# An attention and feed-forward kernel takes x turned by the host in three of four batches

## The chip, the cores and the metric

The kernel runs on one core of one Trainium2 chip. The metric is the device time of one execution in microseconds. Before the change the median of 3 runs is 2160.63 us (2160.58 to 2162.61). The engines are TensorE (PE; PEld is its weight load), VectorE (DVE), ScalarE (ACT), GpSimd (POOL) and SyncE (SP, which here only issues DMAs).

## The reference

x is 4 batches of 512 rows of 1024. Each batch attends to itself and to 64 rows of context, and a feed-forward block with a router follows. Cut to what matters here:

```python
m = jnp.mean(x, axis=-1, keepdims=True)            # _layernorm, per row of x
v = jnp.var(x, axis=-1, keepdims=True)
z = (x - m) / jnp.sqrt(v + 1e-5)
q = z @ Wq.T                                       # 16 heads of 96
hidden = jnp.concatenate([context, z], axis=1)
k, v = hidden @ Wk.T, hidden @ Wv.T                # 4 key and value heads of 96
x = x + softmax(q k^T / sqrt(96)) v @ Wo.T
x = x + ffn(layernorm(x))                          # up, relu^2, down; a routed low-rank path
```

Mean and root belong to a row of x, that is to a token.

## The kernel before

TensorE contracts over partitions, so z must stand with features on partitions and tokens along the free dimension. Every product is made of three fp32r matmuls (`parts3`, lines 116 to 118) of operands split in a high and a low part; for z these are `zhi` and `zlo`, 8 chunks (k) of 128 features by 512 tokens.

The program runs in stages: p0 (weights are split, the context is projected, batch 0 is normalized), a (projections of each batch), b (attention), c, d and e. The change is in stage a. There, for each batch, PE makes 19 output chunks (A_EV): 3 of k and 12 of q, each 128x512, in five groups of three (k index outside, chunk inside), and then 4 value tiles t of 128x384. A group uses three PSUM banks, and two sets of banks alternate. Each chunk n is evicted by ACT (`a_hi_out`, line 527) and DVE (`a_lo_out`, line 532) into one of two staging slots and stored by SP (`a_store`, line 547). ACT waits until the slot's last stores have landed.

z of batch b + 1 is made inside batch b. SP loads x (2 MB, line 153) early in batch b, with tokens on partitions. Ahead of chunk 9's eviction DVE takes statistics, the root (with ACT's square root) and scales x in place to z (lines 177 to 198). PE turns z in 8 blocks of four 128x128 transposes (`pe_t`, line 210): two blocks ahead of value tile 2 and the other six behind the k steps 2 to 7 of value tile 3. ACT copies each turned bank to zhi (line 219), once the last reader of that part of zhi has passed (semaphore `a_zfree`), and DVE makes zlo (line 223). ACT and DVE do k = 0 to 6 ahead of the last chunk's (18) eviction and k = 7 behind it. PE's next batch waits for zlo of each k, and its second chunk waits until chunk 18 is evicted, whose bank it takes. Each engine's order is written out by hand, and semaphores alone tie the engines together.

In the names of the tiles, "operands" holds weights, zhi, zlo and one staging slot, "staging" holds x, raw weights and the other slot, "small" holds statistics.

## Time and profile before

| what | us |
|---|---|
| median of 3 runs | 2160.63 |
| profiled execution, its own time | 2160.62 |
| its span | 2158.8 |
| PE busy | 2129.8 (99%) |
| DVE busy | 804.3 (37%) |
| ACT busy | 692.2 (32%) |
| POOL busy | 698.7 (32%) |

The span runs from the first to the last instruction of the profiled execution. Matmuls are pipelined: the start of one to the start of the next is its cost, and the duration shown is longer. In stage a, POOL has no instruction from 100 to 350 us.

### The profile page before, as it was taken

The page shows a single profiled execution, that of the slowest core. Times are in us where ns is not written, and L with a number is a line of the kernel's source. Part 1 is how long each engine was busy: PE and PEld are TensorE (multiplying, and loading weights), DVE is VectorE, ACT ScalarE, POOL GpSimd, SP SyncE. Part 2 cuts the span into 40 slices and gives each one's busy share as a digit, 9 for nine tenths or more (in the row PEclk, how much of TensorE's full clock was granted, in tenths as well). Part 3 has the DMA queues.
Part 4 walks back from the last instruction along what each step waited for, and adds up shares of the span by engine and source line. Part 5 has one row for each costly group of instructions (what it writes and reads, how often), then busy time and mean ns, then how long its engine had stood idle before and what let it go on. Part 6 is the DMA issues. An engine that isn't in the chain of part 4 may idle for free.

```text
span 2158.8 us, 30561 instructions
## 1 busy us (share of the span) xinstructions
PE 2129.8 (99%) x9820; PEld 1752.6 (81%) x9820; DVE 804.3 (37%) x1407; ACT 692.2 (32%) x1201; POOL 698.7 (32%) x572
## 2 busy tenths in 40 slices
PE   7999999999999999999999999999999999999998
PEld 6888888887777777878888878788888888888886
DVE  4223222167777778850100313232221132222222
ACT  4111111047777777761111223211123311111111
POOL 3500000126777767672222434010004422222221
PEclk9999999999999999999999999999999999999999
DMA  4732322525556556534333535322114532222222
GB/s 165 233 127 107 126 97 88 164 85 140 141 144 162 136 134 156 131 96 149 134 119 119 187 103 173 110 78 97 63 66 138 188 109 81 86 84 88 84 87 72
DMA packets 230940, 261.62 MB, mean 121 GB/s; under 512 B 76496, under 2 KB 144336, under 8 KB 230736
## 3 DMA queue, kind: packets, MB, share of 16 engines
q1 hardware_dynamic: 186016, 188.70, 28.6%
q10 hardware_dynamic: 44848, 71.97, 10.9%
q8 instruction: 40, 0.66, 0.1%
q14 instruction: 36, 0.29, 0.1%
HBM read 168.07 MB, written 92.27 MB: 121 GB/s over the span
## 4 chain that ended last, share of the span: by engine, by line
PE 97%; DVE 1%; DMA 1%; issue 1%; ACT 0%; POOL 0%; SPq 0%; DVEq 0%; ACTq 0%; POOLq 0%
PE psum L116 30%; PE psum L117 29%; PE psum L118 29%; PE psum L865 3%; PE psum L210 1%; PE psum L916 1%; PE psum L917 1%; PE psum L900 1%; PE psum L899 1%; DMA staging<-in_wqkv 1%; PE psum L1530 0%; PE psum L1529 0%; PE psum L872 0%; DVE staging L198 0%; DMA staging<-in_ctx 0%
## 5 line engine op out<-in xcount | busy, mean ns | idle before, releaser
L116 PE MATMUL psum<-operands 128*128 128x512 f32 (+3 forms) x2888 | 1125.0, 390 | 12.2 <-DVE operands L325 9.1
L117 PE MATMUL psum<-operands 128*128 128x512 f32 (+3 forms) x2888 | 1111.1, 385 | 0.0
L118 PE MATMUL psum<-operands 128*128 128x512 f32 (+3 forms) x2888 | 1109.7, 384 | 0.0
L116 PEld LDWEIGHTS psum<-operands 128*128 128x128 f32 (+1 forms) x2888 | 543.9, 188 | 119.4 <-DVE operands L325 10.2
L118 PEld LDWEIGHTS psum<-operands 128*128 128x128 f32 (+1 forms) x2888 | 544.3, 188 | 106.7
L117 PEld LDWEIGHTS psum<-operands 128*128 128x128 f32 (+1 forms) x2888 | 545.2, 189 | 92.9
L1158 POOL TENSOR_TENSOR operands<-staging,operands 128x512 fp32r<-128x512 f32 x92 | 118.3, 1296 | 367.7 <-ACT operands L1153 367.4
L1044 DVE TENSOR_REDUCE small<-psum 128x1 f32<-128x576 f32 x256 | 192.1, 750 | 99.7 <-PE psum L865 99.7
L1757 POOL TENSOR_TENSOR operands<-operands 128x640 fp32r<-128x640 f32 x64 | 100.6, 1578 | 318.8 <-ACT operands L1752 318.7
L786 POOL TENSOR_TENSOR operands<-staging,operands 128x512 fp32r<-128x512 f32 x128 | 164.0, 1289 | 36.1 <-ACT operands L966 27.3
L1609 DVE TENSOR_TENSOR staging<-staging 128x512 f32<-128x512 f32 x64 | 46.0, 738 | 304.3 <-ACT staging L1575 303.5
L1752 ACT ACTIVATE operands<-operands 128x640 fp32r<-128x640 f32 x64 | 47.3, 740 | 282.4 <-DMA operands<-h_scratch 282.4
L1344 POOL TENSOR_TENSOR operands<-operands 128x384 fp32r<-128x384 f32 x64 | 66.0, 1037 | 183.1 <-ACT operands L1339 182.5
L779 POOL MEMSET operands<- 64x32 f32 (+7 forms) x22 | 8.6, 389 | 350.4 <-PE psum L118 349.3
L959 ACT ACTIVATE staging<-psum 128x512 f32<-128x512 f32 (+1 forms) x192 | 109.3, 588 | 39.4 <-DVE psum L1072 33.0
L865 PEld LDWEIGHTS psum<-operands 96*128 96x128 f32 x512 | 91.0, 189 | 33.6 <-DVE small L1044 17.9
L865 PE MATMUL psum<-operands 96*128 96x288 f32 x512 | 116.2, 309 | 0.3 <-DVE small L1044 0.3
L966 ACT ACTIVATE operands<-staging 128x512 fp32r<-128x512 f32 (+1 forms) x192 | 112.9, 620 | 0.0
L788 POOL TENSOR_TENSOR operands<-staging,operands 64x512 fp32r<-64x512 f32 x64 | 82.5, 1288 | 74.0 <-ACT operands L966 70.4
L1153 ACT ACTIVATE operands<-staging 128x512 fp32r<-128x512 f32 x92 | 56.3, 629 | 140.0 <-DMA staging<-in_up_w 57.7
L1575 ACT ACTIVATE staging<-psum 128x512 f32<-128x512 f32 x80 | 46.5, 597 | 165.2 <-PE psum L118 159.7
L532 DVE SCALAR_TENSOR_TENSOR staging<-psum,staging 128x512 fp32r<-128x512 f32 (+1 forms) x40 | 26.5, 664 | 192.5 <-ACT staging L527 192.5
(102 smaller groups left out, 1363.6 us busy)
## 6 DMA issues: line engine op xcount, KB each, us to landing
h_scratch<-staging ACTq DMA_DIRECT2D x80, 256.0 KB, 2.1
operands<-h_scratch SPq DMA_DIRECT2D x64, 320.0 KB, 3.1
operands<-recip_scratch SPq DMA_DIRECT2D x64, 192.0 KB, 4.1
o_scratch<-staging SPq DMA_DIRECT2D x64, 192.0 KB, 4.8
operands<-o_scratch SPq DMA_DIRECT2D x64, 192.0 KB, 2.7
operands<-q_hi_scratch ACTq DMA_DIRECT2D x14, 768.0 KB, 5.9
operands<-q_lo_scratch ACTq DMA_DIRECT2D x14, 768.0 KB, 5.8
staging<-in_x SPq DMA_DIRECT2D x20, 512.0 KB, 3.9
```

Of the source, the lines that this page charges most:

```text
L116: e.matmul(o, lh, rh, start=first, stop=False)
L117: e.matmul(o, lh, rl, start=False, stop=False)
L118: return e.matmul(o, ll, rh, start=False, stop=last)
L786: e.tensor_tensor(pt[j][1], pst[j // 2], raw(pt[j][0]), ALU.subtract).then_inc(b_lop, 1)
L788: e.tensor_tensor(pt[j][0][C:P], pst[j // 2][0:C], raw(pt[j][0][0:C]), ALU.subtract).then_inc(b_lop, 1)
L865: m = e.matmul(bank[:, h * TH:(h + 1) * TH], qp[p][0][0:HD, a * S + u * P:a * S + (u + 1) * P], kp[p][0][0:HD, h * TH:(h + 1) * TH], start ...
L959: e.activation(pst[j // 2][0:n], bank[0:n], ACT.Exp).then_inc(b_ex, 1)
L966: e.activation(pt[j][0][0:n], pst[j // 2][0:n], ACT.Copy).then_inc(b_hia, 1)
L1044: e.tensor_reduce(nm[o % 2][:, u:u + 1], bank[:, 0:T], AX.X, ALU.max, negate=True).then_inc(b_mx, 1)
L1158: e.tensor_tensor(job_part(j, h, slot_lo), halves[h], raw(job_part(j, h, slot_hi)), ALU.subtract).then_inc(j_lo, 1)
L1344: e.tensor_tensor(cu[u][1], raw(cu[u][1]), raw(cu[u][0]), ALU.subtract).then_inc(cc_lo, 1)
L1757: e.tensor_tensor(eu[u][1], raw(eu[u][1]), raw(eu[u][0]), ALU.subtract).then_inc(e_lo, 1)
```

## The change

The host hands over a second copy of x, `xt`, with features on partitions (128 partitions, 8 chunks k, 512 tokens). Batch 0 is made as before. For batches 1 to 3:

- x is still loaded with tokens on partitions, four neighbouring tokens to each partition, and DVE takes mean and root from it. It no longer scales x, but copies the mean to its own place (line 199 of the changed kernel).
- SP, behind chunk 9's stores, loads the batch's part of `xt` (2 MB) over x and stores the mean and the root (2 KB each) to DRAM. Behind chunk 10's stores it waits for these to land and loads them back spread over all partitions (MR, 128x1024).
- GpSimd subtracts the mean and multiplies by the root in place, 16 operations of 128x512.
- ACT makes zhi (line 499) and DVE makes zlo (line 503) from there; PE does no turning.

```diff
@@ -148,15 +149,15 @@
             def load(e, src, b):
-                e.wait_ge(*past(zt, b * DK))
+                e.wait_ge(*past(zl if tiles else zt, b * DK))
                 e.sem_inc(idle, 1)
-                e.dma_start(xn, src[bass.ds(b * S, S), :].rearrange("(t p) d -> p t d", p=P)).then_inc(ld, 16)
+                e.dma_start(xn, src[bass.ds(b * S, S), :].rearrange("(p t) d -> p t d" if tiles else "(t p) d -> p t d", p=P)).then_inc(ld, 16)
             def load_tile(e, src, t):
                 e.dma_start(xn[:, t, :], src[t * P:(t + 1) * P, :]).then_inc(ld_t[t], 16)
-            def dve_norm(e, b, by_tile=None):
+            def dve_norm(e, b, by_tile=None, z=True):
                 n = [0]
                 def link(ins, last=True):
@@ -194,9 +195,12 @@
                 link(e.tensor_scalar(n1, n1, -0.5, 1.5, ALU.mult, ALU.add))
                 link(e.tensor_tensor(rstd, n1, rt, ALU.mult))
                 assert n[0] == LN_CHAIN
+                if not z:
+                    e.tensor_copy(mean, mv[:, :, 0]).then_inc(cp, 1)
+                    return
                 for t in range(ST):
-                    z = e.tensor_scalar(xn[:, t, :], xn[:, t, :], mv[:, t, 0:1], rstd[:, t:t + 1], ALU.subtract, ALU.mult)
-                z.then_inc(zn, 1)
+                    m = e.tensor_scalar(xn[:, t, :], xn[:, t, :], mv[:, t, 0:1], rstd[:, t:t + 1], ALU.subtract, ALU.mult)
+                m.then_inc(zn, 1)
             def act_sqrt(e, b, to=rt):
                 e.wait_ge(*past(ch, b * LN_CHAIN + 14))
@@ -269,6 +273,11 @@
         c_stage = [tuple(mmf(10 * SLOT + (2 * c + i) * BC, BC) for i in range(2)) for c in range(KC)]
         c_stage += [tuple(mmf(11 * SLOT + (2 * t + i) * KVE, KVE) for i in range(2)) for t in range(2)]
         stage = [tuple(SF[:, STG + i * NB:STG + (i + 1) * NB].bitcast(f32r) for i in range(2)), (mmf(GWO, NB), mmf(GWO + NB, NB))]
+        XT = SF[:, 0:DK * S].rearrange("p (k s) -> p k s", k=DK)
+        mean = sm[:, 320:320 + ST]
+        MR = SF[:, STG + 2 * NB:STG + 4 * NB]
+        a_ms, a_mr, a_xt = sem("a_moments_stored", 32), sem("a_moments_spread"), sem("a_x_turned")
+        a_sub, a_mul = sem("a_mean_off"), sem("a_normalized", DK)
         c_mm, c_sh, c_ev, c_st = (sem(f"ctx_{n}") for n in ("product", "staged_hi", "staged", "stored"))
         v_w = [MM[:, 15 * SLOT:18 * SLOT].rearrange("p (c h k e) -> p h k c e", c=KC, h=2, k=DK)[:, i] for i in range(2)]
         v_rows = [t.rearrange("(q s) d -> q s d", s=T) for t in v_d]
@@ -440,8 +449,58 @@
         A_GROUPS = [[QC, QC + 1, QC + 2]] + [[3 * g, 3 * g + 1, 3 * g + 2] for g in range(QC // 3)]
         NQK = QC + KC
         A_EV = NQK + ST
-        a_load, a_load_tile, a_norm, a_sqrt, a_pet, a_hi, a_lo, a_zl, a_fr, a_zt = norm_z(
+        a_load, a_load_tile, a_norm, a_sqrt, a_pet, a_hi, a_lo, a_zl, a_fr, a_zt, a_zh, a_ch, a_cp = norm_z(
             "a", XN, lambda e, b: e.wait_ge(*past(a_acc, b * A_EV)), (5, 6, 7), True)
+
+        A_CP = 1
+
+        def a_moments_out(e, b):
+
+            e.wait_ge(*past(a_ch, b * LN_CHAIN + 2 * ST))
+            e.sem_inc(idle, 1)
+            e.dma_start(XT, xt.rearrange("b p k s -> (b p) k s")[bass.ds(b * P, P)]).then_inc(a_xt, 16)
+            e.wait_ge(*past(a_ch, b * LN_CHAIN + LN_CHAIN))
+            e.sem_inc(idle, 1)
+            e.wait_ge(*past(a_cp, b + A_CP))
+            e.sem_inc(idle, 1)
+            for q, src in enumerate((mean, rstd)):
+                e.dma_start(m_d[q * S:(q + 1) * S].rearrange("(p t) -> p t", t=ST), src).then_inc(a_ms, 16)
+
+        def a_moments_in(e, b):
+
+            if isinstance(b, int):
+                e.wait_ge(*past(w_lop, len(BY_POOL) + 2 * QC))
+            e.wait_ge(*past(a_mul, b * DK - DK))
+            e.sem_inc(idle, 1)
+            e.wait_ge(*past(a_ms, b * 32))
+            e.sem_inc(idle, 1)
+            e.dma_start(MR, m_d.partition_broadcast(P)).then_inc(a_mr, 16)
+
+        def a_pool(e):
+            def take_mean(k):
+                e.tensor_tensor(XT[:, k, :], XT[:, k, :], MR[:, 0:S], ALU.subtract).then_inc(a_sub, 1)
+
+            with e.Fori(1, B) as b:
+                e.wait_ge(*past(a_xt, b * 16))
+                e.wait_ge(*past(a_mr, b * 16))
+                take_mean(0)
+                for k in range(DK):
+                    if k + 1 < DK:
+                        take_mean(k + 1)
+                    e.wait_ge(*past(a_sub, b * DK + (k + 1 - DK)))
+                    e.tensor_tensor(XT[:, k, :], XT[:, k, :], MR[:, S:2 * S], ALU.mult).then_inc(a_mul, 1)
+
+        def a_hi_next(e, b, k):
+            e.wait_ge(*past(a_mul, b * DK + (k + 1 - DK)))
+            if k < DK - 1:
+                e.wait_ge(*past(a_fr, (b - 1) * (DK - 1) + k + 1))
+            else:
+                e.wait_ge(*past(a_acc, b * A_EV))
+            e.activation(zhi[:, k, :], XT[:, k, :], ACT.Copy).then_inc(a_zh, 1)
+
+        def a_lo_next(e, b, k):
+            e.wait_ge(*past(a_zh, b * DK + k + 1))
+            e.tensor_tensor(zlo[:, k, :], XT[:, k, :], raw(zhi[:, k, :]), ALU.subtract).then_inc(a_zl, 1)
         def a_sp(e):
             more = [[13], [14, 15, 16], [17, 18], [19, 20], [21, 22], [23]]
@@ -449,6 +508,10 @@
                 a_store(e, 0, n)
                 if n == 3:
                     a_load(e, x_r, 1)
+                if n == 9:
+                    a_moments_out(e, 1)
+                if n == 10:
+                    a_moments_in(e, 1)
                 for k in [NF + q for q in (more[n] if n < len(more) else [])]:
                     c, h = LATER[k - NF]
                     if (c, h) == (8, 0):
@@ -482,9 +549,6 @@
                     g, c = t // 2, t % 2
                     if c == 0:
                         e.wait_ge(*past(a_ev, b * A_EV + 3 * (len(A_GROUPS) - 1 + g)))
-                    if t == ST - 2 and not last:
-                        a_pet(e, b + 1, 0)
-                        a_pet(e, b + 1, 1)
                     for k in range(DK):
                         zt_ = [z[:, k, t * P:(t + 1) * P] for z in (zhi, zlo)]
                         m = parts3(e, PS[:, 3 * ((g + 1) % 2) + c, 0:KVE], zt_[0], zt_[1],
@@ -495,8 +559,6 @@
                             m.then_inc(a_acc, 1)
                         elif t == ST - 1:
                             m.then_inc(a_fr, 1)
-                        if t == ST - 1 and k >= 2 and not last:
-                            a_pet(e, b + 1, k)
             e.wait_ge(*past(c_ev, KC))
             with e.Fori(0, B - 1) as b:
@@ -553,13 +615,13 @@
                         a_sqrt(e, b + 1)
                     if n == A_EV - 1 and not last:
                         for k in range(DK - 1):
-                            a_hi(e, b + 1, k)
+                            a_hi_next(e, b + 1, k)
                     a_hi_out(e, b, n)
                     if n == A_EV - 3 and last:
                         e.wait_ge(*past(ph_start, 2))
                         e.activation(sm[:, 336:337], ident[:, 0:1], ACT.Exp)
                 if not last:
-                    a_hi(e, b + 1, DK - 1)
+                    a_hi_next(e, b + 1, DK - 1)
             with e.Fori(0, B - 1) as b:
                 body(b, False)
@@ -569,15 +631,16 @@
             def body(b, last):
                 for n in range(A_EV):
                     if n == 9 and not last:
-                        a_norm(e, b + 1)
+                        e.wait_ge(*past(a_ms, b * 32))
+                        a_norm(e, b + 1, z=False)
                     if n == A_EV - 1 and not last:
                         for k in range(DK - 1):
-                            a_lo(e, b + 1, k)
+                            a_lo_next(e, b + 1, k)
                     a_lo_out(e, b, n)
                     if last and NQK <= n < A_EV - 1:
                         b_dve_first(e, n - NQK + 1)
                 if not last:
-                    a_lo(e, b + 1, DK - 1)
+                    a_lo_next(e, b + 1, DK - 1)
             with e.Fori(0, B - 1) as b:
                 body(b, False)
@@ -2003,6 +2067,7 @@
     arrays = {
         "x": inputs["x"],
+        "xt": np.asarray(inputs["x"]).reshape(-1, 512, 8, 128).transpose(0, 3, 2, 1),
         "ctx": in_rows(np.asarray(inputs["ctx_4096"]).reshape(-1, inputs["ctx_4096"].shape[-1]).T, 1).reshape(128, 8, -1),
         "wqkv": in_chunks(np.concatenate([np.asarray(inputs[_P + w]) for w in ("Wq", "Wk", "Wv")], axis=0).T),
         "wo": np.asarray(inputs[_P + "Wo"]).T,
```

On PE, at the end of a batch's loop body, before. Tile 3's k steps end in blocks of turns of the z in "staging", each waiting for the PSUM bank (`a_zlo`); L502 is the loop's branch:

```order
L116 MATMUL psum<-operands 128x384
L117 MATMUL psum<-operands 128x384
L118 MATMUL psum<-operands 128x384
L208 REGISTER_ALU
L210 MATMUL psum<-ident,staging 128x128 [waits a_zlo]
L210 MATMUL psum<-ident,staging 128x128 x3
L502 REGISTER_ALU
L502 COMPARE_AND_BRANCH
```

And in the changed kernel, where the products that follow are the next group's first chunks (512 wide); the second chunk's first product waits for the evictions alone (`a_staged`):

```order
L117 MATMUL psum<-operands 128x384
L118 MATMUL psum<-operands 128x384
L119 MATMUL psum<-operands 128x384
L564 REGISTER_ALU
L564 COMPARE_AND_BRANCH
L117 MATMUL psum<-operands 128x512 [waits a_staged,a_zlo]
L118 MATMUL psum<-operands 128x512
L119 MATMUL psum<-operands 128x512
L117 MATMUL psum<-operands 128x512 [waits a_staged]
```

Eight blocks of turns per body are gone, two of them ahead of tile 2, and nothing stands in their place.

On DVE, at the same place, before: chunk 17's eviction and the first zlo, seven of which stand there ahead of chunk 18's eviction:

```order
L532 SCALAR_TENSOR_TENSOR operands<-psum,operands 128x384 [waits a_staged_hi]
L222 ISA
L223 TENSOR_TENSOR operands<-psum,operands 128x512 [waits a_zhi]
L222 REGISTER_ALU
L223 TENSOR_TENSOR operands<-psum,operands 128x512 [waits a_zhi]
```

And in the changed kernel:

```order
L594 SCALAR_TENSOR_TENSOR operands<-psum,operands 128x384 [waits a_staged_hi]
L502 ISA
L503 TENSOR_TENSOR operands<-staging,operands 128x512 [waits a_zhi]
L502 REGISTER_ALU
L503 TENSOR_TENSOR operands<-staging,operands 128x512 [waits a_zhi]
```

The order is the same; the subtraction reads x from "staging" where it read a PSUM bank.

On GpSimd, between the weight split and stage b, a loop body over batches 1 to 3 is new. Its start (L481 takes the mean off, L491 multiplies by the root):

```order
L481 TENSOR_TENSOR staging<-staging 128x512 [waits a_moments_spread,a_x_turned]
L481 TENSOR_TENSOR staging<-staging 128x512
L490 ISA
L491 TENSOR_TENSOR staging<-staging 128x512 [waits a_mean_off]
L481 TENSOR_TENSOR staging<-staging 128x512
L490 REGISTER_ALU
L491 TENSOR_TENSOR staging<-staging 128x512 [waits a_mean_off]
```

It begins with both loads' landing; the multiplication for k stands one subtraction behind its own. ACT's zhi for k waits for it (`a_normalized`).

## Rows read from the trace of the kernel before

**Rows 1.** The page, part 4: the chain that ended last, by engine.
```profile
PE 97%; DVE 1%; DMA 1%; issue 1%; ACT 0%; POOL 0%; SPq 0%; DVEq 0%; ACTq 0%; POOLq 0%
```

**Rows 2.** PE in order of time: start, duration, engine, line, count [idle before].
```profile
235.07 1.03 PE L210 MATMUL psum<-ident,staging 128*128 128x128 f32 x8
235.86 0.42 PE L116 MATMUL psum<-operands 128*128 128x384 f32 x1
...
240.11 0.33 PE L116 MATMUL psum<-operands 128*128 128x384 f32 x1
...
240.63 0.33 PE L116 MATMUL psum<-operands 128*128 128x384 f32 x1
...
247.52 0.61 PE L210 MATMUL psum<-ident,staging 128*128 128x128 f32 x4
248.06 0.49 PE L116 MATMUL psum<-operands 128*128 128x512 f32 x1
...
249.12 0.50 PE L116 MATMUL psum<-operands 128*128 128x512 f32 x1
```

**Rows 3.** DVE in order of time, statistics and turnover of the same batch.
```profile
206.22 2.98 DVE L198 TENSOR_SCALAR staging<-staging,small 128x1024 f32<-128x1024 f32 x4 [0.15 <-DVE small L195]
...
240.91 0.56 DVE L532 SCALAR_TENSOR_TENSOR operands<-psum,operands 128x384 fp32r<-128x384 f32 x1 [4.48 <-ACT operands L527]
241.46 1.29 DVE L223 TENSOR_TENSOR operands<-psum,operands 128x512 fp32r<-128x512 f32 x2
```

**Rows 4.** SP in order of time: stores of chunks 9 and 11.
```profile
211.25 0.38 SPq L547 DMA_DIRECT2D q_lo_scratch<-operands  x1
...
215.08 0.33 SPq L547 DMA_DIRECT2D q_hi_scratch<-operands  x1
```

**Rows 5.** DMA issues of the whole span: count, KB each, median us to landing.
```profile
staging<-in_x SPq DMA_DIRECT2D x3, 2048.0 KB, 7.9
q_hi_scratch<-staging SPq DMA_DIRECT2D x24, 256.0 KB, 2.1
...
staging<-in_gamma SPq DMA_DIRECT2D x1, 512.0 KB, 4.7
staging<-in_beta SPq DMA_DIRECT2D x1, 512.0 KB, 4.2
```

**Rows 6.** DMA issues between 74 and 90 us.
```profile
staging<-in_x SPq DMA_DIRECT2D x1, 2048.0 KB, 11.0
...
q_hi_scratch<-staging SPq DMA_DIRECT2D x1, 256.0 KB, 9.3
```

**Rows 7.** POOL in order of time, two operations with DVE quiet.
```profile
1603.56 2.55 POOL L1158 TENSOR_TENSOR operands<-staging,operands 128x512 fp32r<-128x512 f32 x2 [28.34 <-ACT operands L1153]
```

**Rows 8.** POOL and DVE in order of time, in stage p0.
```profile
19.20 8.38 POOL L325 TENSOR_TENSOR operands<-staging,operands 128x512 fp32r<-128x512 f32 x6 [14.10 <-ACT operands L320]
...
23.64 5.21 DVE L198 TENSOR_SCALAR staging<-staging,small 128x1024 f32<-128x1024 f32 x4
```

**Rows 9.** Line 1704 (ns min/median/max), and POOL and DVE beside it.
```profile
L1704 DVE TENSOR_TENSOR operands<-staging,operands x12: 677/692/2070, 1720.8 to 1735.5; 128x512 fp32r<-128x512 f32 x12
...
1719.34 3.57 POOL L1757 TENSOR_TENSOR operands<-operands 128x640 fp32r<-128x640 f32 x2 [4.64 <-ACT operands L1752]
...
1720.78 8.15 DVE L1704 TENSOR_TENSOR operands<-staging,operands 128x512 fp32r<-128x512 f32 x8 [4.93 <-ACT operands L1698]
```

**Rows 10.** Line 1067, subtractions from PSUM in stage b (ns min/median/max).
```profile
L1067 DVE TENSOR_TENSOR operands<-psum,operands x128: 691/692/692, 459.0 to 959.1; 128x512 fp32r<-128x512 f32 x128
```

**Rows 11.** PE after idles; then slices: us, PE, PEld, DVE, ACT, POOL busy, PEclk, DMA, GB/s.
```profile
23.13 0.41 PE L116 MATMUL psum<-operands 128*128 128x384 f32 x1 [2.00 <-POOL operands L325]
...
28.91 2.82 PE L210 MATMUL psum<-ident,staging 128*128 128x128 f32 x12 [3.46 <-DVE staging L198]
...
28.00:30.00 2.00, 1.09 (x5) 1.09 (x6) 0.85 (x2) 0.00 (x0) 0.00 (x0) 0.53 0.08 25
...
34.00:36.00 2.00, 2.00 (x14) 1.87 (x12) 0.88 (x3) 0.78 (x2) 0.00 (x0) 0.76 0.00 0
```

More of the change, by code:

```diff
@@ L3, with xattn_ffn_kernel @@
 from contextlib import ExitStack
-def xattn_ffn_kernel(nc, x, ctx, wqkv, wo, gate_w, up_w, down_w, fc1_w, fc2_w, expert_w, gamma, beta, out):
+def xattn_ffn_kernel(nc, x, xt, ctx, wqkv, wo, gate_w, up_w, down_w, fc1_w, fc2_w, expert_w, gamma, beta, out):
     f32 = mybir.dt.float32
@@ L53, in xattn_ffn_kernel @@
     w_d = dram("fold_scratch", (L, D))
+    m_d = nc.dram_tensor("moments_scratch", (2 * S,), f32, kind="Internal").ap()
     x_r = x.rearrange("b s d -> (b s) d")
@@ L223, in dve_lo @@
                 e.tensor_tensor(zlo[:, k, :], z_bank(b, k), raw(zhi[:, k, :]), ALU.subtract).then_inc(zl, 1)
-            return load, load_tile, dve_norm, act_sqrt, pe_t, act_hi, dve_lo, zl, fr, zt
+            return load, load_tile, dve_norm, act_sqrt, pe_t, act_hi, dve_lo, zl, fr, zt, zh, ch, cp
         def mm_groups(e, b, groups, lo_sem, wait_bank, slot_of, done, slot_ready=None, after_group=None, free=None, pe_t=None):
@@ L463, in a_sp @@
                     a_store(e, b, n)
+                    if n == 9:
+                        a_moments_out(e, b + 1)
+                    if n == 10:
+                        a_moments_in(e, b + 1)
         def a_pe(e):
@@ L1207, in xattn_ffn_kernel @@
         d_acc = sem("d_product", 20)
-        d_load, _, d_norm, d_sqrt, d_pet0, d_hi, d_lo, d_zl, d_fr, d_zt = norm_z(
+        d_load, _, d_norm, d_sqrt, d_pet0, d_hi, d_lo, d_zl, d_fr, d_zt, _, _, _ = norm_z(
             "d", XN2, lambda e, b: e.wait_ge(*past(d_acc, b * ND)))
@@ L1930, in _ @@
             a_sp(e)
-            e.wait_ge(*past(a_zt, B * DK))
+            e.wait_ge(*past(a_zl, B * DK))
             e.sem_inc(idle, 1)
@@ L1948, in _ @@
             p0_pool(e)
+            a_pool(e)
             b_pool(e)
```

## The prediction, on record before the changed kernel ran

> **What bounds the kernel now.** I read the chain of waits first: PE is 97% of what ended last [rows 1]. So a change pays only where it takes matmuls away or ends a PE wait, and costs where it makes one. Next I read PE's order of time at a turnover from one batch to the next, the second of the three (loop index 1 to 2, near 240 us) [rows 2], then DVE's at the same place [rows 3]. In them the reader is to see a tight hand-over. PE turns z between its last value products (line 210); ACT copies the turned bank to zhi and DVE subtracts it to zlo; then chunk 18, the batch's last value product, is evicted by ACT and DVE, and the next batch's second chunk may overwrite its bank. That chunk's first product stands at 249.12 us. All times below are of this turnover unless said; the other two repeat it. The profiled execution took 2160.62 us around a span of 2158.8, and the median of the runs is 2160.63, so the sum is made on 2160.6.
>
> **What goes.** PE loses 8 blocks of 4 turns per turnover, 96 turns over three. The first two blocks stand at 235.07 and the products resume at 235.86: 0.79 us, and 0.88 with the slower first product behind them. The value products step 0.52 us per k (240.11, 240.63) [rows 2]. Without turns the last tile (t = 3) starts at 240.11 - 0.88 = 239.2, ends 8 x 0.52 later at 243.4, and the first chunk of the next batch takes its three products with the loop's branch in about 0.9 us (now under 1.25: the last block of turns starts at 247.52, takes 0.36, and 249.12 is the second chunk) [rows 2]. PE therefore reaches the second chunk at 244.3 instead of 249.12. That is the whole possible gain: 4.8 us, 14.5 for three. DVE also loses four 128x1024 scalings, 2.98 us [rows 3], but those lie under products of group 3, where DVE idles; I cost that at nothing.
>
> **What comes.** GpSimd takes 16 operations of 128x512 per batch (8 subtractions of the mean, 8 multiplications by the root); ACT's and DVE's split now reads x from SBUF, not PSUM. When can GpSimd start? DVE has the moments at about 206.4, when now its scaling begins at 206.22 [rows 3], before chunk 9 is evicted. SP issues chunk 9's second store at 211.25 (0.38 us) [rows 4], then the turned x at 212.0. A load of 2 MB lands 7.9 us after its issue [rows 5]: 219.9. The two stores of the moments stand right behind it on the same queue. Behind such a load a store of 256 KB took 9.3 us [rows 6], where that kind's median is 2.1 [rows 5]; so I let the small ones land just after the load, 220.3. SP issues the spread at 220.6. It moves 512 KB, as gamma's (4.7 us) and beta's (4.2) [rows 5]; the middle gives 225.05, so GpSimd starts at 225.1. Two of its operations back to back took 2.55 us, 1.25 for the pace after the first [rows 7]: operation n ends at 225.15 + 1.25n. The multiplication for k is operation 2k + 3, and k = 7's is the 16th, at 245.15.
>
> **Where it meets DVE.** Chunk 17's eviction on DVE stands at 240.91 now [rows 3]; 0.88 earlier, 0.55 us long, it lets DVE ask for its first zlo at 240.6. GpSimd then is in operation 13 of 16. Now DVE reads PSUM and zhi, one SBUF operand, and 128 such subtractions beside a busy GpSimd never took over 692 ns [rows 10]. The new one reads x and zhi, both SBUF. The kernel before has this very form in its last stage: twelve of them took 692 ns in the median and 2070 at most, and beside GpSimd operations eight took 8.15 us and two GpSimd ones 3.57 instead of 3.1 [rows 9]. At the start four DVE scalings took 5.21 us beside GpSimd [rows 8] against 2.98 alone [rows 3], while six GpSimd operations took 8.38, not 7.6. So the two engines take turns there: DVE waits out a GpSimd operation, GpSimd then about 0.5 us of DVE. Worked through:
> - DVE 0 waits to 241.4 and is done at 241.9; GpSimd 14 to 243.15; DVE 1 to 243.65; GpSimd 15 to 244.9; DVE 2 to 245.4; GpSimd 16 to 246.65; DVE 3 to 247.15.
> - GpSimd is out. DVE 4 to 6 go at the pace of the pair in [rows 3], 1.29 less 0.69: 0.60 each, 248.95. Chunk 18's eviction adds 0.55: 249.5.
> ACT is not late: k = 6 is multiplied at 244.9. PE's second chunk starts at 249.5 instead of 249.12: all 4.8 us are gone and 0.4 more. Bounds from the same rows: no blocking gives -3.4 us (below), and rows spread 2.5 us later give +2.7.
>
> The Trainium skill (SBUF — State Buffer, Who interferes with whom) says that a VectorE instruction with two SBUF inputs contends with a GpSimd instruction that reads SBUF, and that whoever issues first has the shared ports for the whole instruction. The trace agrees on the contention [rows 9]. Taken alone the rule would also allow a steady GpSimd to keep DVE out until its 16th operation: then DVE starts at 245.15 and PE at 249.85, 0.7 us late instead of 0.4. The 8.38 us of [rows 8] speak for taking turns, so the sum uses that.
>
> **The new idle time and PE's clock.** Now [rows 2] show no idle of note here. After, PE stands from 244.3 to 249.5, 5.2 us at one stretch. Near 21 us an idle of 2.00 left the next products at full pace; one of 3.46, ending at 28.91, came with a granted clock of 0.53 in the slice 28 to 30 and 0.76 in 34 to 36 [rows 11], so the half level (1.2 GHz of 2.4) held from 28.1 to about 35.0. PE worked 6.1 us at it and lost half: 3.0 us. A stall of 5.2 us is longer than the one that did this, so I take 3.0 us per turnover; bounds 0 (clock stays) and 3.0.
>
> **Waits added elsewhere.** SP waits for the moments' stores after chunk 10. Behind it stand chunk 11's stores, at 215.08 now [rows 4] and at about 221 then. Who waits for those is ACT's eviction of chunk 13, a whole group of 72 products later; nothing is lost unless the load takes over 6 us more. ACT waits for each multiplication with chunk 18's eviction queued behind; that is in the sum. GpSimd's loop lies between its weight split and stage b's fills; DVE's wait for the old stores of moments was met a batch ago. Turned x overwrites x only once the statistics are read. These I cost at nothing; what the added 6 MB of loads cost is in the landing times.
>
> **Sum.** Three turnovers at 0.4 + 3.0 = 3.4 us: +10.2. 2160.6 + 10.2 = 2170.8, so 2171.
>
> **Rivals.**
> 1. The spread rows come later (the small stores or the spread take 2.5 us more behind chunk 10's stores). GpSimd starts at 227.6 and is in operation 11 when DVE asks; five turns instead of three, PE at 251.85: +2.7, and the clock's 3.0. Three times 5.7: 2177.7. For it: the one queue carries all this.
> 2. As forecast, but the clock holds. 3 x 0.4: 2161.8. For it: only one long idle in the middle of work is there to read. Against: it was the shorter one.
> 3. The other side, faster: DVE is not kept out, since its subtraction proceeds beside GpSimd's. Then ACT's k = 6 waits for operation 15 (243.9), is done at 244.5, DVE at 245.1, chunk 18 at 245.7; PE is 3.4 us early and idles 1.5, too short for the clock. 3 x -3.4: 2150.5. Against it [rows 9].
> 4. Also faster: the small stores overtake the 2 MB. The Trainium skill's page DMA: Bandwidth & Descriptors (Queues, rings and completion order) says that completion is not in order per issuing engine; it also says that each DMA engine takes descriptors in ring order, and the 9.3 us of [rows 6] agree with that part. As a mechanism here: the moments land within some 2 us of their issue, the spread shares the load's time and lands near 221.5; GpSimd's 16th operation ends at 241.55, DVE runs free from there (0.5 + 6 x 0.6 + 0.55), PE resumes at 246.25, 2.9 us early with 2 us of idle. 3 x -2.9: 2152. The sign flips where the rows are spread before about 223: each microsecond there is nearly one at PE, and the clock comes or stays with it.
>
> **Chances.** Forecast 0.60, rival 1 0.17, rival 2 0.10, rival 3 0.07, rival 4 0.06. This kernel's measurement tells about 0.2%, 4.3 us. Faster is rivals 3 and 4: 0.13. Within 0.2% is rival 2: 0.10. Slower is the rest: 0.77. The range runs from rival 2's place less its error, 2160, to rival 1's with some more, 2180; outside lie rivals 3 and 4 and some 0.04 beyond rival 1.
>
> **What would show it.** In the profile after: no turns on PE between 40 and 360 us (line 214 there); DVE's line 503 with seven per turnover, the first three or four 1.2 to 1.8 us each while GpSimd's lines 481 and 491 stretch from 1.29 to about 1.75; GpSimd starting some 13 us after the load's issue; one PE idle of 4.5 to 6 us per turnover ended by DVE's eviction (line 594); a granted clock of 0.5 for some microseconds after it, three times. Wrong would be: line 503 flat at 0.69, GpSimd done before 240.6 on this scale, PE idle under 2.5 us, or a clock that stays at 1.00.

## The result, and the profile after

The changed kernel takes 2173.06 us (median of 5 runs, 2170.58 to 2177.88), against 2160.58 us for the kernel before on the same chip (5 runs, 2157.89 to 2162.61): ratio 1.0064, 95% interval 1.0053 to 1.0075. The change makes the kernel 0.6% slower. Its profiled execution took 2175.06 us around a span of 2173.2.

The chain of waits of the changed kernel, against [rows 1]:

```profile
PE 94%; DVE 2%; DMA 1%; issue 1%; ACT 1%; POOL 0%; DVEq 0%; SPq 0%; ACTq 0%; POOLq 0%
```

PE gave up three points of the chain. The waits of PE (line waited for: us in total, times, longest) name whom it waits for:

```profile
PE psum L117 <- DVE staging L594: 12.9, 3, 7.6
PE psum L117 <- DVE operands L334: 9.0, 6, 6.2
PE psum L117 <- DVE operands L503: 6.7, 2, 3.7
```

Line 334 is line 325 of the kernel before, which had 9.1 us there. The other two, five waits and 19.6 us, all stand at the turnovers: 594 is DVE's eviction, here of chunk 18, and 503 the new subtraction. PE in order of time at the first turnover (columns as in [rows 2]):

```profile
140.09 0.39 PE L117 MATMUL psum<-operands 128*128 128x512 f32 x1
...
140.56 0.40 PE L119 MATMUL psum<-operands 128*128 128x512 f32 x1
148.57 0.80 PE L117 MATMUL psum<-operands 128*128 128x512 f32 x1 [7.62 <-DVE staging L594]
149.16 0.63 PE L118 MATMUL psum<-operands 128*128 128x512 f32 x1
```

and at the second, the one of [rows 2]:

```profile
252.96 0.49 PE L117 MATMUL psum<-operands 128*128 128x512 f32 x1 [3.69 <-DVE operands L503]
...
253.53 0.55 PE L119 MATMUL psum<-operands 128*128 128x512 f32 x1
256.96 0.80 PE L117 MATMUL psum<-operands 128*128 128x512 f32 x1 [2.88 <-DVE staging L594]
```

The reader is to see two things. The transposes are gone, and in their place PE stands idle: at the first turnover once, 7.62 us before the second chunk; at the second twice, 3.69 us before the first chunk, whose first zlo is late, and 2.88 before the second chunk (at the third 3.04 and 2.43). And the products behind the idle last longer: 0.63 us where 0.40 stood. Two windows of equal length, one right after the other (busy time and count of each engine, then granted clock, DMA share, GB/s), show what that costs:

```profile
148.60:154.60 6.00, 6.00 (x14) 4.80 (x15) 0.51 (x1) 0.00 (x0) 0.00 (x0) 0.50 0.85 273
154.70:160.70 6.00, 6.00 (x28) 4.96 (x27) 0.00 (x0) 0.00 (x0) 0.00 (x0) 1.00 0.30 128
```

PE is busy in both, at 1.2 GHz with 14 products, at 2.4 GHz with 28.

DVE at the first turnover, against [rows 3]:

```profile
136.73 0.56 DVE L594 SCALAR_TENSOR_TENSOR operands<-psum,operands 128x384 fp32r<-128x384 f32 x1 [3.60 <-ACT operands L589]
137.31 10.73 DVE L503 TENSOR_TENSOR operands<-staging,operands 128x512 fp32r<-128x512 f32 x7
147.97 0.54 DVE L594 SCALAR_TENSOR_TENSOR staging<-psum,staging 128x384 fp32r<-128x384 f32 x1
```

Seven subtractions take 10.73 us. Six of them took 1.75 to 1.77 each, the seventh, with GpSimd done, 0.68. GpSimd beside them:

```profile
137.22 1.30 POOL L491 TENSOR_TENSOR staging<-staging 128x512 f32<-128x512 f32 x1
138.47 1.74 POOL L481 TENSOR_TENSOR staging<-staging 128x512 f32<-128x512 f32 x1
140.17 1.71 POOL L491 TENSOR_TENSOR staging<-staging 128x512 f32<-128x512 f32 x1
```

The two engines take turns here. SP and its landings set when GpSimd starts (SP in order of time at the second turnover, against [rows 4]):

```profile
217.70 0.36 SPq L461 DMA_DIRECT2D staging<-in_xt  x1
218.38 0.81 SPq L467 DMA_DIRECT2D moments_scratch<-small  x2
...
227.74 0.33 SPq L477 DMA_DIRECT2D staging<-moments_scratch  x1
```

To measure a turnover I use two marks: the start of a batch's first value product (128x384), and the first product of the second chunk of the next batch. Before, the value products start at 123.25, 226.73, 330.17 and 433.62, and the second chunk 22.4 us behind each. After, they start at 123.43, 232.45, 339.63 and 447.49, so the turnovers cost 5.54, 3.74 and 4.41 us, 13.7 in all. The second chunk (148.57, 256.96, 363.59) is late against the 22.4 by 2.7, 2.1 and 1.6 us; the remaining 2.8, 1.6 and 2.9 come behind it, while the clock is halved. The profiled execution lies 2.0 us above the median of its runs, so the marks give 13.7 us where the medians give 12.5.

### The profile page after: what moved, and what is told of

It is laid out like the page before. It is cut to its first block, busy times and chain, and to the rows that moved or that the text cites. A ratio compares the mean times of both kernels' runs of the same rounds, so it can differ in the third digit from the quotient of the medians.

```text
span 2173.2 us, 30459 instructions
## 1 busy us (share of the span) xinstructions
PE 2126.0 (98%) x9724; PEld 1748.6 (80%) x9724; DVE 811.1 (37%) x1398; ACT 692.0 (32%) x1201; POOL 760.4 (35%) x620
## 4 chain that ended last, share of the span: by engine, by line
PE 94%; DVE 2%; DMA 1%; issue 1%; ACT 1%; POOL 0%; DVEq 0%; SPq 0%; ACTq 0%; POOLq 0%
PE psum L117 29%; PE psum L118 29%; PE psum L119 28%; PE psum L928 3%; PE psum L214 1%; DMA q_lo_scratch<-operands 1%; PE psum L979 1%; PE psum L980 1%; PE psum L963 1%; PE psum L962 1%; DVE operands L503 1%; DMA staging<-in_wqkv 0%; PE psum L1593 0%; PE psum L1592 0%; PE psum L935 0%
## 5 line engine op out<-in xcount | busy, mean ns | idle before, releaser
L481 POOL TENSOR_TENSOR staging<-staging 128x512 f32<-128x512 f32 x24 | 32.1, 1343 | 197.7 <-DMA staging<-moments_scratch 197.7
```

## The experiments

The times of the kernel before beside the first four are 2159.76 (2158.15 to 2161.15), beside the next four 2160.01 (2158.23 to 2161.02). "Idle" is PE's longest at a turnover by the waits.

**Without GpSimd.** Nothing normalizes x; ACT and DVE wait for the load alone. Its lines 501 and 592 are 503 and 594 of the changed kernel.

```diff
-            e.wait_ge(*past(a_mul, b * DK + (k + 1 - DK)))
+            e.wait_ge(*past(a_xt, b * 16))
...
-            a_pool(e)
```

> The changed kernel with GpSimd's loop left out: ACT and DVE split x as it was loaded, so z is not normalized in batches 1 to 3 (this leaves work out). All loads, stores and the statistics stay. Theory: GpSimd is the whole loss, through its late results and through keeping DVE off; then DVE's seven splits run free, PE reaches the second chunk 3 to 3.5 us earlier than before the change, idles about 1.5 us and keeps its clock: about 2150.5 us. Rival: the loss is in reading x from SBUF or in the added loads and SP's waits: 2160 or more.

2148.3 us (2147.72 to 2150.47), ratio 0.9948 [0.9934, 0.9961]: 2 us under what I had expected. DVE in order of time:

```profile
234.25 4.30 DVE L501 TENSOR_TENSOR operands<-staging,operands 128x512 fp32r<-128x512 f32 x7
```

and PE:

```profile
237.03 0.39 PE L117 MATMUL psum<-operands 128*128 128x512 f32 x1
...
239.07 0.50 PE L117 MATMUL psum<-operands 128*128 128x512 f32 x1 [1.18 <-DVE staging L592]
```

Seven subtractions take 4.30 instead of 10.73 us, the idle is 1.2, the clock stays at 1.00 from 110 to 380 us, and a batch takes 99.75 us where before took 103.45. All of the loss hangs on GpSimd, and so do the 3.7 us per turnover that the missing transposes can give. This run alone can't say whether GpSimd's lateness or its use of SBUF does it.

**Data apart.** ACT and DVE split rows of the weights in place of x; GpSimd's work goes on beside them, and neither waits for it (only SP does, before it loads the next batch's x).

```diff
-            e.wait_ge(*past(a_mul, b * DK + (k + 1 - DK)))
...
-            e.tensor_tensor(zlo[:, k, :], XT[:, k, :], raw(zhi[:, k, :]), ALU.subtract).then_inc(a_zl, 1)
+            e.tensor_tensor(zlo[:, k, :], raw(slot_hi(k)[:, 0:NB]), raw(zhi[:, k, :]), ALU.subtract).then_inc(a_zl, 1)
```

> The changed kernel, where GpSimd does its 16 operations at the same times on the turned x, but nobody waits for them: ACT and DVE split other data in SBUF (parts of the weights, so the output is not that of the reference). Theory (DVE is kept off while GpSimd reads SBUF): DVE's first splits of a turnover still take several us, PE's idle stays 5 to 8 us and its clock halves, 2169 to 2176 us. Rival (GpSimd's results are late, and ACT waits for them): DVE's splits take 0.68 us and the time falls to about 2150.

2172.11 us (2170.99 to 2177.16), ratio 1.0067 [1.0053, 1.008]. DVE in order of time:

```profile
136.03 9.73 DVE L502 TENSOR_TENSOR operands<-operands 128x512 fp32r<-128x512 f32 x7
```

and GpSimd:

```profile
136.16 1.75 POOL L481 TENSOR_TENSOR staging<-staging 128x512 f32<-128x512 f32 x1
137.87 1.75 POOL L491 TENSOR_TENSOR staging<-staging 128x512 f32<-128x512 f32 x1
```

With no wait between them, four or five subtractions per turnover still take 1.74 to 1.79 us, PE idles 6.9 us at most and the clock halves three times. Contention while both run is enough for the whole loss; that GpSimd's results are late is not needed for it. What late results would cost without the contention is not shown: no run has the one without the other.

**Three chunks earlier.** Statistics, load, stores and spread move from chunks 9 and 10 to 6 and 7, on SP, ACT and DVE.

```diff
-                if n == 9:
+                if n == 6:
-                if n == 10:
+                if n == 7:
```

> The changed kernel with statistics, the turned load and the moments' stores at chunk 6 and the spread at chunk 7, one group (16.3 us) earlier, nothing else. Theory: GpSimd is through about 10 us before tile 3, so neither late results nor shared access remain: each turnover gains 3 to 3.5 us against the kernel before, 2150 to 2152 us, with no slice at half clock there. Rival: loads at that time hold up the stores of chunks 6 to 8 and PE's banks: over 2155.

2148.98 us (2148.43 to 2149.5), ratio 0.9951 [0.9937, 0.9964], 1 us under the range that I gave. The last two GpSimd operations before the second turnover:

```profile
221.50 2.54 POOL L491 TENSOR_TENSOR staging<-staging 128x512 f32<-128x512 f32 x2
```

and DVE:

```profile
234.18 4.30 DVE L503 TENSOR_TENSOR operands<-staging,operands 128x512 fp32r<-128x512 f32 x7
```

GpSimd is done 10 us before DVE asks, and the kernel is as fast as without GpSimd. GpSimd starts 16.3 us ahead of the batch's value products here (204.0 against 220.3), instead of about at them; the same work is free there. At the first turnover it starts 7.6 us ahead, and that was enough too: the batch takes the same 99.76 us.

**Filler.** 20 products into an unused bank behind the value products keep PE busy where it would stand. It tells the clock's share.

```diff
+                if not last:
+                    for i in range(20):
+                        e.matmul(PS[:, 7, :], slot_hi(QC)[:, 0:P], slot_hi(QC + 1)[:, 0:NB], start=True, stop=True)
```

> The changed kernel with 20 single matmuls of 512 columns (4.5 us) into an unused bank behind each of the first three batches' last value product, whose results nobody reads. They fill most of the stall. Theory: the half clock is about 8.5 of the 12.5 us lost (6.05, 3.5 and 7.5 us of PE's work at half level in the profile after). The clock stays full in the two shorter stalls at least, and the time falls to 2163 to 2167. Rival: the clock doesn't matter or falls anyway, and the fillers add where the stall is shorter than they are: 2173 or more.

2168.2 us (2166.32 to 2170.05), ratio 1.0041 [1.0027, 1.0054]: between what I had expected and the rival. PE at the first turnover:

```profile
146.26 0.50 PE L117 MATMUL psum<-operands 128*128 128x512 f32 x1 [2.28 <-DVE staging L597]
...
146.83 0.40 PE L119 MATMUL psum<-operands 128*128 128x512 f32 x1
```

PE in order of time, second turnover:

```profile
243.98 4.74 PE L564 MATMUL psum<-operands 128*128 128x512 f32 x20
...
251.21 0.50 PE L117 MATMUL psum<-operands 128*128 128x512 f32 x1 [1.81 <-DVE staging L597]
...
251.82 0.63 PE L119 MATMUL psum<-operands 128*128 128x512 f32 x1
```

and three windows, one per turnover:

```profile
140.00:160.00 20.00, 17.72 (x79) 14.33 (x78) 6.81 (x7) 1.89 (x4) 4.59 (x3) 1.00 0.36 125
245.00:262.00 17.00, 15.19 (x61) 12.06 (x60) 6.75 (x7) 1.64 (x3) 3.93 (x3) 0.90 0.40 147
350.00:368.00 18.00, 16.57 (x74) 13.42 (x73) 7.89 (x8) 2.28 (x4) 5.07 (x3) 1.00 0.12 25
```

The clock now holds at two turnovers of three, the first and the third, and the turnovers cost 1.9, 3.1 and 1.2 us against before: 6.2 instead of 13.7. That is 7.5 less in the traces, but the medians gained only 4.9. The second chunk is late by 2.0, 1.5 and 1.1 us here, which is 1.8 less in all than in the changed kernel. What comes behind it is 0.0, 1.6 and 0.0 instead of 2.8, 1.6 and 2.9: where the clock holds, this part is gone, 5.7 us. So the halved clock follows what PE does in the gap, not the absence of the transposes. The length of an idle alone does not tell which level comes: 2.28 us at the first turnover and 1.43 at the third left the clock full, 1.81 at the second did not. Why is open.

**Moments first.** The two small stores stand ahead of the load of x.

```diff
-            e.dma_start(XT, xt.rearrange("b p k s -> (b p) k s")[bass.ds(b * P, P)]).then_inc(a_xt, 16)
...
+            e.dma_start(XT, xt.rearrange("b p k s -> (b p) k s")[bass.ds(b * P, P)]).then_inc(a_xt, 16)
```

> The changed kernel with one exchange on SP: the two small stores of mean and root are issued ahead of the 2 MB load of turned x instead of behind it. Theory (the end of GpSimd's work against the turnover decides): the small stores no longer wait out the load (they landed 8.5 us after issue), the spread is issued right behind chunk 10's stores, shares the queue with the load, and lands about 2 us behind it: GpSimd starts about 11 us after the load's issue instead of 14 to 15.6, DVE meets its last two operations at most, PE idles about 3 us: each turnover 1 to 2 us ahead of the kernel before if the clock holds: 2154 to 2158. Rival (order of the small stores doesn't matter, since the queue finishes them with the load anyway): within 2 us of the changed kernel, 2171 to 2175.

2169.95 us (2169.59 to 2171.08), ratio 1.0046 [1.0033, 1.006]: I was wrong by 12 us or more. DMA issues between 105 and 125 us (count, KB each, us to landing), this kernel:

```profile
staging<-in_xt SPq DMA_DIRECT2D x1, 2048.0 KB, 9.2
...
staging<-moments_scratch SPq DMA_DIRECT2D x1, 512.0 KB, 9.2
moments_scratch<-small SPq DMA_DIRECT2D x2, 2.0 KB, 2.4
```

and the changed kernel, same stretch:

```profile
staging<-in_xt SPq DMA_DIRECT2D x1, 2048.0 KB, 10.5
...
staging<-moments_scratch SPq DMA_DIRECT2D x1, 512.0 KB, 4.4
moments_scratch<-small SPq DMA_DIRECT2D x2, 2.0 KB, 8.5
```

The small stores land in 2.4 us instead of 8.5, as I had expected; but now the spread is issued while the load runs and takes 9.2 us instead of 4.4. GpSimd starts 11.9 us after the load's issue in the first turnover instead of 15.6, and 11.5 instead of 14.6 in the second. Part of that is given back, since the load itself is issued later: 13.7 us ahead of the value products instead of 14.75 in the second turnover, behind the small stores. (In the first the load's place varies from trace to trace of the changed kernel, 14.3, 12.1 and 12.5 us ahead; here it is 11.8.) In its batch GpSimd starts 1.3, 2.1 and 1.4 us sooner than in the first trace of the changed kernel. PE still idled 4.5 to 6.5 us, with the clock halved three times.

**A busy GpSimd beside the kernel before.** 20 multiplications of 128x512 per turnover (line 456) run beside DVE's old subtraction.

```diff
+                e.wait_ge(*past(a_acc, b * A_EV + NQK))
+                for j in range(20):
...
+                    e.tensor_tensor(SF[:, to:to + NB], raw(slot_hi(13)[:, 0:NB]), raw(slot_hi(14)[:, 0:NB]), ALU.mult).then_inc(a_busy, 1)
```

> The kernel before the change, with 20 GpSimd multiplications of 128x512 added at each of the three turnovers (from chunk 14's product on), which read weights and write to unused room in SBUF. DVE's splits read PSUM there. Theory (only a DVE operation with two operands in SBUF is kept off): DVE's line 223 stays at 0.69 us and the time is that of before, within 1.5 us: 2158 to 2162. Rival (GpSimd's mere activity in the turnover slows DVE or PE): 2165 or more.

2159.8 us (2159.08 to 2160.84), ratio 1.0000 [0.9991, 1.0009]. Groups of instructions (busy, mean ns, idle before):

```profile
L456 POOL TENSOR_TENSOR staging<-operands 128x512 f32<-128x512 f32 x60 | 74.9, 1294 | 181.0 <-PE psum L118 181.0
L223 DVE TENSOR_TENSOR operands<-psum,operands 128x512 fp32r<-128x512 f32 x64 | 43.4, 689 | 55.6 <-ACT operands L219 55.6
```

and the same two groups of the changed kernel, where DVE reads two operands from SBUF:

```profile
L491 POOL TENSOR_TENSOR staging<-staging 128x512 f32<-128x512 f32 x24 | 32.4, 1360 | 0.0
L503 DVE TENSOR_TENSOR operands<-staging,operands 128x512 fp32r<-128x512 f32 x24 | 32.4, 1407 | 0.1
```

With one operand in PSUM neither engine notices the other (689 and 1294 ns). It is the change of DVE's operand, not GpSimd's work as such, that makes them meet.

**Eviction sooner.** As three chunks earlier, and chunk 18's eviction stands behind four splits instead of seven.

```diff
-                        for k in range(DK - 1):
+                        for k in range(4):
...
-                    a_lo_next(e, b + 1, DK - 1)
+                    for k in range(4, DK):
+                        a_lo_next(e, b + 1, k)
```

> The kernel of e3 (all of the added work one group earlier) with chunk 18's eviction moved on ACT and DVE from behind the split of k = 6 to behind that of k = 3. Theory: the idle of 1.36 us that e3 still has at each turnover is DVE's chain of seven splits ahead of that eviction; with four ahead, the eviction waits for PE's product itself and PE idles about 0.5 us: 0.9 us less each, 2146 to 2147 against e3's 2149. Rival (zlo of k = 4 to 7, now later, holds PE up in turn): no gain or a loss.

2148.03 us (2146.04 to 2150.32), ratio 0.9942 [0.9928, 0.9955], 1 us above the range that I gave. PE:

```profile
240.72 0.51 PE L117 MATMUL psum<-operands 128*128 128x512 f32 x1 [0.55 <-DVE staging L594]
```

The idle falls from 1.19 to 0.55 us, the batch from 99.75 to 99.1.

**Second chunk last.** In addition PE takes the second chunk after the third at the first k of the first group.

```diff
-                    for c, ch in enumerate(chunks):
+                    for c, ch in [list(enumerate(chunks))[q] for q in ((0, 2, 1) if swap and g == 0 and k == 0 else (0, 1, 2)[:len(chunks)])]:
```

> The kernel of e7 where PE, in a batch's first group, takes at k = 0 the third chunk before the second, whose bank is the last to be evicted. Theory: 0.7 us of products cover what idle e7 leaves; the three turnovers have no idle, 1 to 1.5 us less than e7 in all: 2144.5 to 2146.

2147.01 us (2145.7 to 2149.71), ratio 0.9942 [0.9928, 0.9955]: 13 us under the kernel before, and again 1 above the range that I gave. A batch takes 98.45 us, 5.0 less than before. No idle is left at the turnovers. In the medians the last two steps (1 us each) lie within the spread of the runs; only the marks in the traces show them apart.

**The changed kernel twice more.** In its first trace the second turnover read otherwise than the first. DVE and GpSimd, this trace:

```profile
246.34 10.11 DVE L503 TENSOR_TENSOR operands<-staging,operands 128x512 fp32r<-128x512 f32 x7
```

```profile
246.03 1.32 POOL L481 TENSOR_TENSOR staging<-staging 128x512 f32<-128x512 f32 x1
247.28 1.32 POOL L491 TENSOR_TENSOR staging<-staging 128x512 f32<-128x512 f32 x1
248.53 1.31 POOL L481 TENSOR_TENSOR staging<-staging 128x512 f32<-128x512 f32 x1
249.76 2.52 POOL L491 TENSOR_TENSOR staging<-staging 128x512 f32<-128x512 f32 x2
```

GpSimd is hardly slowed; DVE's first subtraction took 6.50 us, its end 0.56 behind that of GpSimd's last operation, and the others 0.68. The third was the same, with 5.93.

> The changed kernel once more, for a second trace. Open is why in its first trace VectorE and GpSimd took turns in the first turnover (six subtractions of 1.75 us) and VectorE was kept out in the other two (first subtraction 6.50 and 5.93 us, then 0.68 each). Theory A, it is the moment at which VectorE asks that decides, which varies by a fraction of a microsecond from execution to execution: then the pattern changes, kept out in another number or other places of the three, and the time lies within 2170 to 2178 us. Theory B, it is fixed by the place in the loop: again turns in the first turnover and kept out in the second and third.

> The same kernel a third time, for a third trace. Theory A (the moment of asking decides): the pattern of turns and of kept out need not be that of either trace before, and over nine turnovers both kinds occur. Theory B (the place in the loop decides): first turnover turns, second and third kept out, as before. Time 2170 to 2178 us by both.

2179.34 and 2175.33 us, one run each; the first lies above the 2178 that I had given. All six turnovers took turns, the second ones too (first the one trace, then the other):

```profile
245.67 9.40 DVE L503 TENSOR_TENSOR operands<-staging,operands 128x512 fp32r<-128x512 f32 x7
```

```profile
245.46 9.71 DVE L503 TENSOR_TENSOR operands<-staging,operands 128x512 fp32r<-128x512 f32 x7
```

So the place in the loop does not decide: of nine turnovers seven took turns and two kept DVE out. The moment of asking, which was my other theory, does not sort them either: in the two, DVE asked 0.3 and 0.9 us into a GpSimd operation; in the seven, 0.1 us into one, twice 0.4 and four times 1.2 (and in the data apart once 0.8). What does tell them apart in these traces is GpSimd's own pace before DVE asks. In the two its operations last 1.32 us on average from the third on, in the seven 1.29 (first trace, second turnover; then the second trace's):

```profile
241.04 1.32 POOL L481 TENSOR_TENSOR staging<-staging 128x512 f32<-128x512 f32 x1
```

```profile
241.55 1.29 POOL L491 TENSOR_TENSOR staging<-staging 128x512 f32<-128x512 f32 x1
```

The nine turnovers of the data apart, of the filler and of the moments first all took turns, with 1.29 as well. This goes along with the pattern; no run varied it, so what decides stays open.

At the first turnover of both new traces DVE also waited for ACT, and ACT for GpSimd's product:

```profile
147.41 1.00 DVE L503 TENSOR_TENSOR operands<-staging,operands 128x512 fp32r<-128x512 f32 x1 [1.89 <-ACT operands L499]
```

GpSimd starts latest there (+2.7 us), and its late results show beside the contention, as they do not in DVE's rows of the first trace.

The three traces together, and the one with the moments first, give what I had wanted from the prediction's sum: GpSimd's start against the batch's first value product, and how late the second chunk is (us).

```
                      taking turns: start -> late          DVE kept out
changed, 1st trace    +1.3 -> 2.7                          -0.1 -> 2.1   -0.7 -> 1.6
changed, 2nd trace    +2.8 -> 4.0   -0.2 -> 1.4   +0.2 -> 1.8
changed, 3rd trace    +2.7 -> 3.9   +0.3 -> 1.7   -0.3 -> 1.3
moments first          0.0 -> 1.6   -2.2 -> -0.4  -2.2 -> -0.3
```

Where they take turns the second chunk moves by 0.9 us per us of start ((4.0 + 0.4) / (2.8 + 2.2)). Where DVE is kept out it is some 0.6 later than that line.

## Why the prediction was right, point by point

**Direction and time.** 2171 was forecast with 0.77 on slower; 2173.06 was measured, well inside 2160 to 2180. The mechanism is the one forecast (DVE held up by GpSimd, then a stall of PE, then its halved clock); the sizes are not.

**What goes.** PE could reach the second chunk 4.8 us sooner, and a version in which nothing kept DVE out would gain 3.4 per turnover: without GpSimd it is 3.7, and with the eviction and the order mended 5.0.

**GpSimd's start: mis-sized.** In the second turnover SP issued the load 14.75 us before the batch's value products, as forecast (212.0 against 226.73). From there I had 13.1 us; it was 15.6, 14.6 and 14.0 in the first trace. The load took 8.9 to 10.5 us, not the 7.9 of [rows 5] ([rows 6] had one of 11.0), and the second small store landed 9.6 to 11.0 us behind its issue, not 8.3; the spread's 4.2 to 4.4 was right. So GpSimd started at -0.1 in the second turnover where the sum had 225.1 - 226.73 = -1.6. The table's line at -1.6 gives 0.1 to 0.2 us late, close to the 0.4 of the sum: the working from start to stall was sound, its input was off. That is rival 1's mechanism at part of its size, and it is why the second chunk is 2.7, 2.1 and 1.6 us late, not 0.4.

**Taking turns.** Pairs of 1.75 us, as taken from [rows 8], hold in seven turnovers of nine (from one subtraction's start to the next, after the first, 1.66 to 1.71). But five to seven subtractions were held up, not four, since GpSimd started later. The Trainium skill (SBUF — State Buffer, Who interferes with whom) lets whoever issues first have the shared ports for a whole instruction; the 6.50 us of the second turnover are what that rule allows if GpSimd issues first each time, and the 1.75 us are what it allows if they alternate. I had set the first aside on one row, and it happened twice; I had it cost 0.3 us more than taking turns, and it was some 0.6.

**The clock: right in kind, somewhat large in size.** I took 3.0 us per turnover and 9.0 in all; 2.8, 1.6 and 2.9 were measured, 7.3. Two of them are as forecast; at the second turnover PE worked only 3.5 us at the half level behind the second chunk, not 6.1. The filler run shows that this part goes when PE is kept busy in the gap. Rival 2, a clock that holds, is refuted by the windows above.

**The sum.** Predicted 1.2 + 9.0 = 10.2; measured 6.4 + 7.3 = 13.7 in the trace. The two misses partly cancel, which made the total look better than its terms: that the clock cost 1.7 us less than forecast, where the second chunk's lateness cost 5.2 more, is luck.

**Rivals 3 and 4.** DVE not kept out is refuted by line 503's 1407 ns, and the data apart shows that no wait hides behind them. Small stores that overtake by much do not occur (8.5 us): of the two, one landed up to 1.0 us ahead of the load, as at 333.02 against 333.90, but never the second, and the spread waits for both. The run that puts them first shows more: even then GpSimd starts only 1.3 to 2.1 us sooner in its batch, because the spread then takes 8.4 to 9.2 us in their place. The sign flip that I had put at 223 (-3.7) is not contradicted: at -2.2 PE's second chunk was already 0.4 early and the turnover still cost 1.6 to 2.0 us, since its idle kept halving the clock; at -7.6 and -16 (three chunks earlier) it gained. Between -2.2 and -7 no run lies.

**Costs of nothing.** SP's later stores and DVE's missing scalings cost or gave nothing that any trace shows: the run without GpSimd keeps both, and its batches are 3.7 us shorter, about the 4.8 us of transposes less the 1.2 of idle.

**The signs.** GpSimd started 14.0 to 15.6 us after the load's issue, where I had named some 13. The idle was in one piece and ended by line 594 only at the first turnover of the first trace, where it was 7.6 us and not 4.5 to 6; at the other two line 503 ended a first piece, which I had not foreseen: with DVE kept out, even the next batch's first zlo is late.

## What to carry to other kernels

Here work moved to an idle engine was free while its memory accesses did not meet those of the engine that feeds TensorE. So ask which operands the neighbour reads from SBUF, and finish the moved work before the hand-over, not beside it. The same instructions cost 0.6% at one place and gave 0.5% three chunks earlier. A stall of TensorE of 4.5 us and more was paid twice here, once as idle and once as what the halved clock took from the products behind it; at about 2 us it went both ways.

## What the runs showed of the hardware that was not expected

Between a back-to-back GpSimd and a VectorE that both read from SBUF there are two patterns, in one and the same kernel: turns, in which an instruction of either takes 1.70 to 1.79 us, or VectorE kept out for 5.9 to 6.5 us with GpSimd at 1.30 to 1.34. Which of them comes varies between executions of one kernel. A TensorE idle of 1.81 us was followed by the half clock where one of 2.28 in the same execution was not. A store of 2 KB behind a load of 2 MB on its queue took 8.5 us, ahead of it 2.4; the 512 KB behind it then took 9.2 instead of 4.4.
